# A decoder of five attention and feed-forward stages: constant matmuls as the second stage begins, its loads issued in two places, and the fifth stage's statistics in its loop

## The reference

```python
x = x + _L0_attn_ref(_layernorm(x, axis=-1), ...)
x = x + _L0_xattn_ref(_layernorm(x, axis=-1), ctx_512, ctx_512)
x = x + _L0_ffn_ref(_layernorm(x, axis=-1), ...)
x = x + _L1_attn_ref(_layernorm(x, axis=-1), ...)
x = x + _L1_xattn_ref(_layernorm(x, axis=-1), ctx_512, ctx_512, ...)
x = x + _L1_ffn_ref(_layernorm(x, axis=-1), ...)
```

## Time and profile before

| | us |
|---|---|
| median of three runs | 1947.82 |
| the profiled execution | 1944.22 |
| its span, first to last instruction | 1942.4 |
| TensorE busy | 1711.3 (88%) |
| VectorE busy | 1134.2 (58%) |
| ScalarE busy | 842.3 (43%) |
| GpSimd busy | 686.1 (35%) |
| mean granted TensorE clock | 0.902 |

### The profile page before, as it was taken

One profiled execution on the slowest core, in us unless ns is written; L12 is line 12 of the kernel. 1 busy time (PEld: TensorE's weight loads), 2 busy tenths in 40 slices (PEclk: granted clock), 3 DMA queues, 4 the chain that ended last, 5 costly groups with the idle time before them and its releaser, 6 DMA issues. The chain is left out here.

```text
span 1942.4 us, 33715 instructions
## 1 busy us (share of the span) xinstructions
PE 1711.3 (88%) x12986; PEld 1324.9 (68%) x12986; DVE 1134.2 (58%) x1820; ACT 842.3 (43%) x1399; POOL 686.1 (35%) x508
## 2 busy tenths in 40 slices
PE   4999999999959996889999786899998297999997
PEld 3888888888846665668788562444444275788886
DVE  6676767676765555565322495999897666211111
ACT  3555555555533433444422325555562275322222
POOL 0111221122123431640122204999996341223232
PEclk9999999999975555789999896999999598899999
DMA  3011111111120002000000000000000440000001
GB/s 94 15 58 55 63 38 57 54 62 38 57 98 2 1 2 92 2 2 2 2 1 1 19 18 0 1 1 1 0 1 0 157 146 2 1 1 1 1 0 43
DMA packets 49490, 57.56 MB, mean 30 GB/s; under 512 B 7216, under 2 KB 43568, under 8 KB 49248
## 3 DMA queue, kind: packets, MB, share of 16 engines
q1 hardware_dynamic: 49376, 55.97, 8.9%
HBM read 41.28 MB, written 14.68 MB: 29 GB/s over the span
## 5 line engine op out<-in xcount | busy, mean ns | idle before, releaser
L543 POOL TENSOR_TENSOR s_w_parts<-s_w_raw,s_w_parts 128x768 fp32r<-128x768 f32 x16 | 29.7, 1854 | 428.8 <-ACT s_w_parts L495 428.8
L1293 DVE TENSOR_TENSOR s6f_hid<-s6f_act_sb,s6f_u_ps 128x512 f32<-128x512 f32 x64 | 44.0, 687 | 219.5 <-PE s6f_u_ps L1244 219.5
L1316 POOL TENSOR_TENSOR s6f_hid_parts<-s6f_hid,s6f_hid_parts 128x512 fp32r<-128x512 f32 x64 | 82.7, 1293 | 230.5 <-ACT s6f_hid_parts L1282 230.5
L1826 POOL TENSOR_TENSOR s4b_pcs<-s4b_cs,s_p_rows 128x1024 f32<-128x1024 f32 x64 | 120.8, 1913 | 95.4 <-ACT s4b_cs L1872 95.4
L1837 POOL TENSOR_TENSOR s4b_with_re<-s4b_with_re,s4b_with_im 128x1024 f32<-128x1024 f32 x64 | 150.9, 2385 | 2.6 <-DVE s4b_with_im L1791 2.6
L1912 PE MATMUL s4b_c_ps<-s4b_pcs,const 128*128 128x512 f32 x256 | 122.3, 600 | 0.0
L419 PE MATMUL s_v_ps<-s_wv_parts,s_xnT 128*128 128x256 f32 x768 | 103.8, 285 | 12.0 <-ACT s_v L524 6.4
L478 PE MATMUL s_o_ps<-s_w_parts,s_zT 128*128 128x256 f32 x768 | 110.2, 294 | 4.1 <-DVE x_rows L582 4.1
L419 PEld LDWEIGHTS s_v_ps<-s_wv_parts,s_xnT 128*128 128x128 f32 x768 | 96.3, 191 | 17.6 <-ACT s_v L524 9.7
L1902 PE MATMUL s4b_turns_ps<-s_theta_bd,s_zc 128*128 128x512 f32 x128 | 78.1, 694 | 31.4 <-DVE s4b_frac L1776 30.4
L1316 POOL TENSOR_TENSOR s3f_hid_parts<-s3f_hid,s3f_hid_parts 128x512 fp32r<-128x512 f32 x32 | 41.3, 1291 | 180.2 <-ACT s3f_hid_parts L1282 180.2
(11 more groups left out here) (305 smaller groups left out, 4138.4 us busy)
## 6 DMA issues: line engine op xcount, KB each, us to landing
stored_weights<-s1q_halves SPq DMA_DIRECT2D x16, 768.0 KB, 3.5
s6w_parts<-stored_weights SPq DMA_DIRECT2D x32, 384.0 KB, 7.5
s1q_packed<-in_codes SPq DMA_DIRECT2D x8, 384.0 KB, 4.3
s1q_scale<-in_scale_rows SPq DMA_DIRECT2D x8, 384.0 KB, 5.0
x_rows<-in_x SPq DMA_DIRECT2D x1, 2048.0 KB, 8.2
s_w_raw<-in_L_attn_W_Q SPq DMA_DIRECT2D x16, 128.0 KB, 2.2
s_w_raw<-in_L_attn_W_K SPq DMA_DIRECT2D x16, 128.0 KB, 2.4
s_w_raw<-in_L_attn_W_O SPq DMA_DIRECT2D x16, 128.0 KB, 2.4
```

Source lines behind the costliest of these rows:

```text
L1293: nc.vector.tensor_tensor(hid[:, f % 2, :], act_sb[:, f % 2, :], u_ps[:, f % 2, :], ALU.mult) \
L1316: nc.gpsimd.tensor_tensor(hid_parts[:, f % 2, 1, :], hid[:, f % 2, :], hid_parts[:, f % 2, 0, :], ALU.subtract).then_inc(low_done, 1)
L1826: last = nc.gpsimd.tensor_tensor(pcs[:, half, n_, :].rearrange("p (k c) -> p k c", k=HK), cs[:, half, n_, :].rearrange("p (k c) -> p k c", ...
```

## The change

Three edits. `load_context` takes a range of chunks: the statistics block now issues chunk 0, and SyncE issues the chunks 1 to 3 in the main block of the second stage. TensorE's list in the second stage gets a part `keep_busy` at two places: ahead of all others at lag 2, with four matmuls for unit 0, and behind `scores` at lag 3, with one matmul each for the units 0 and 1. Each multiplies the constant `ident` (128x128) with the constant `age` (128x512) in float32 into `o_ps`, where nothing reads it. VectorE's list in the fifth stage gets a part `gather_stats` at lag 6, and `core.stats_ready` is set after that stage.

```diff
@@ -625,8 +625,8 @@
         loads = oroom.sems("in0", "in1", "in2", "in3")
         (zeroed,) = oroom.sems("zeroed")
 
-        def load_context(sp):
-            for n in range(NT // CHUNK):
+        def load_context(sp, first=0, last=1):
+            for n in range(first, last):
                 tiles = slice(n * CHUNK, (n + 1) * CHUNK)
                 sp.dma_start(krep[:, tiles, :, :, :].rearrange("p t r b s -> p t (r b s)"),
                              ins["ctx_rep4"][tiles, :, :].rearrange("t p n -> p t n")).then_inc(loads[n], 16)
@@ -665,6 +665,10 @@
             def attended_of():
                 return o_ps[:, 0:HEADS * (E + 1)].rearrange("p (h e) -> p h e", e=E + 1)
 
+            @block.sync
+            def _(sp):
+                load_context(sp, 1, NT // CHUNK)
+
             @block.gpsimd
             def _(pool):
                 pool.wait_ge(zeroed, 1)
@@ -763,6 +767,14 @@
             @block.tensor
             def _(pe):
                 pe.wait_ge(zeroed, 1)
+
+                def keep_busy(first, later):
+                    def part(u, rnd, n):
+                        if not isinstance(u, int) or u > 1:
+                            return
+                        for _ in range(later if u else first):
+                            nc.tensor.matmul(o_ps[:, :], core.c("ident"), core.c("age"), start=True, stop=True)
+                    return part
 
                 def turn_x(u, rnd, n):
                     i, r, k = u // 2, u % 2, u // 2 % 2
@@ -820,7 +832,7 @@
                             last.then_inc(o_full, 1)
                     return part
 
-                run_steps(pe, U, [(scores, 3), (weigh(0), 5), (turn(0), 4), (weigh(1), 5), (turn(1), 4),
+                run_steps(pe, U, [(keep_busy(4, 0), 2), (scores, 3), (keep_busy(1, 1), 3), (weigh(0), 5), (turn(0), 4), (weigh(1), 5), (turn(1), 4),
                                   (turn_x, 2)], unroll=2, head=U + 5)
 
 
@@ -944,7 +956,12 @@
                     dve.wait_ge(f_full, i + 1)
                     nc.vector.tensor_tensor(core.x[:, i, :], core.x[:, i, :], f_rows, ALU.add).then_inc(f_out, 1)
 
-            steps(dve, [(attended, 4), (shift, 2)] + ([(spread_values, 1)] if own else []) + [(finish, 5)])
+            def gather_stats(i, rnd, k):
+                dve.wait_ge(f_out, i + 1)
+                nc.vector.bn_stats(core.stats[:, i, :], core.x[:, i, :])
+
+            steps(dve, [(attended, 4), (shift, 2)] + ([(spread_values, 1)] if own else []) + [(finish, 5)] +
+                  ([] if own else [(gather_stats, 6)]))
 
         @block.gpsimd
         def _(pool):
@@ -2074,6 +2091,7 @@
 
         attention16(core, "L1", "s5a", mv, rstd, factor, {"q_cos": q_cos[:, :], "q_sin": q_sin[:, :], "shift": shift, "keys": keys, "wo": wo, "values": vbd},
                     prefetch=prefetch)
+        core.stats_ready = True
 
 
 
```

## The result

| | before | after |
|---|---|---|
| median, us | 1948.60 (4 runs, 1945.99 to 1949.42) | 1877.89 (4 runs, 1874.93 to 1880.98) |
| profiled execution, its span | 1944.22, 1942.4 | 1874.93, 1873.1 |
| mean granted clock | 0.902 | 0.952 |

What follows compares the result with a forecast made beforehand. TensorE at half clock (1.2 GHz) was taken to bound the second stage. -54.5 - 3.0 + 0.4 + 0.2 - 4.5 = -61.4 from 1944.22 gave 1882.8, carried to the median 1886; range 1874 to 1938.

Steps and rivals of the forecast that it cites:

- The clock holds: Second stage: TensorE's clock rises to 2.4 GHz and stays there to the end; chance 0.64, own range 1875 to 1898.
- the main term: Second stage's steady loop: 14.5 tile periods at full clock take 108.8 us instead of 163.3, a gain of 54.5.
- rival two: Second stage: clock never rises for the loop, or falls in the gap after the first scores; 1944 us, chance 0.17.
- the rule on transposes: The Trainium skill's rule that transposes don't count as TensorE being busy; the warm second stage would fall back, 1943 us.
- The size of a tile: Second stage's loop at full clock: 3.5 + 4.0 = 7.5 us a tile of two units, against 11.26; bounds 6.8 and 8.4.
- Filling and draining: Second stage outside the steady loop: 19.5 us, of which 3 are saved, between 0 and 6.5.
- The matmuls behind the scores: One constant matmul after each of the second stage's first two scores, mostly hidden while TensorE waits; cost 0.4 us.
- The four first: Constants ahead of the second stage's first transposes: clock rises within them, they end 4.9 to 6.5 us after beginning.
- The statistics: Fifth stage's statistics move into its loop: 5.32 - 0.75 = 4.6 us saved, taken as 4.5 (3.5 to 4.7).
- The view of before as one speed: Kernel before taken at 1944 us, its second stage at half clock; once fallen, the clock would stay down.
- Rival three: Second stage doesn't begin earlier and the constants are dead weight at 1.2 GHz: +2.5, 1950 us; chance 0.05.

Runs made afterwards that it cites:

- e5: The changed kernel with the four constant matmuls first but none behind the scores; 1937.88 us.
- e8: The changed kernel with 32 transposes of a constant in place of the first four constant matmuls; 1879.66 us.
- e6: The changed kernel without the first four constant matmuls, keeping the two behind the scores; 1877.18 us.
- e12: The kernel of e10 without the four constant matmuls at the start of the second stage; 1877.12 us.
- e11: As e1, with six constant matmuls of 256 columns ahead of the scores of units 16 and 17, in the middle of the second stage; 1917.01 us.
- e1: The changed kernel without any constant matmuls, loads and statistics as changed; 1940.65 us.
- e4: The kernel before with only the loads issued in two places; 1951.02, 1949.32, 1883.97 and 1879.79 us.
- the long runs: Executions of the unchanged kernel before: the four in the table and 22 of 33 beside the experiments, which took 1945.9 to 1952.6 us.
- the quick runs: The 11 of 33 executions of the unchanged kernel before, beside the experiments, that took 1882.7 to 1891.2 us (median 1887.2).
- e2: The kernel before with only the constant matmuls added, loads and statistics as before; 1888.13 us.
- e10: The changed kernel plus a 128-column constant matmul behind each tile's transposes, from the seventh tile, in four blocks that split x ahead of a stage; 1877.03 us.
- e9: The changed kernel run once more, unaltered; 1880.29 us.
- e7: The changed kernel with two constant matmuls instead of four ahead of the first transposes; 1878.57 us.

## Why the prediction was right, and where it was off

**The clock holds.** Right as to the time, the main term and the range (1886 against 1877.89; the sum against the profiled execution 1882.8 against 1874.93). That the times could be compared so was partly luck: had the four runs of before in the table been quick ones, the same change would have measured some 0.5%, and nothing of the main term. The gap that rival two named, put at about 1.9 us, was 1.68, and the clock held through it; without the matmul in it, it is 2.73 us, and the clock fell (e5). The weight given to the rule on transposes, little, was right (e8).

**The size of a tile** is the term that was mis-sized: 7.5 us forecast, 7.13 measured, over 14.5 tiles 5.4 of the 8 us by which the time was missed. The odd unit came as worked out (3.42 for 3.4, rounded up to 3.5). The even one was put at 4.0 for a delay in ScalarE's queue, and is 3.71: ScalarE had been idle 1.84 us when the transposes of x were done, so its copy stood behind nothing. Without the two roundings the same rows gave 7.2.

**Filling and draining** brought 4.0 us (182.78 - 118.88 = 63.9, less 14.5 x 4.13 = 59.9), net of what the two matmuls behind the scores cost; 3.0 - 0.4 = 2.6 had been forecast.

**The matmuls behind the scores** cost nothing: the first four scores follow each other every 3.42 us. The 0.4 forecast for them was too much.

**The four first** lasted 6.17 us, within the 4.9 to 6.5 forecast, and the first scores came at 578.50 in a stage that began 1.1 us later than in the trace of before (reciprocal at 571.06 against 569.95). So the start lost 0.88 - 1.11 = -0.2 us, inside -0.7 to +0.9. But the prediction took it that the clock must be up before the first transposes, and that the four bring it up. They did (576.67), but that it must be so was wrong, and the time of the changed kernel couldn't show it: e6 and e12 do without them, in eight executions of eight. So part of this was luck: what the kernels that are quick every time share is that the gaps behind the first two scores are filled, and the prediction counted these two matmuls mainly as a cost of 0.4 us.

**The statistics:** 4.6 us (7.29 to 2.65, from the last add to the square root), which the prediction worked out and took as 4.5. The -4.55 of the whole stage is the difference of two executions: over all traces that stage is 124.8 to 127.2 us with the edit and 129.5 to 130.4 without.

**The view of before as one speed.** The prediction called 1944 the time of the kernel before, and for rival two said that once down the clock stays down. But the stage has two steady speeds (e11), and which of them it gets isn't settled by its instructions (e1 and e4). The median of three runs didn't show that; a dozen very likely would have. The rival's time was right for the long runs only. Against the quick runs the change brings 1887.2 - 1877.9 = 9.3 us, of which e2's 2.6 for the loads and the 4.6 of the statistics are 7.2.

**Rival three** didn't come: GpSimd began at 572.08 and the clock was up before the first transposes.

What stays open: what decides, without the constants, between the two speeds; and the 3 to 4 us by which the third and fourth stages, which no edit touches, differ between executions (417.4 to 421.7 us for the fourth), which is why e10 against e9 can't be settled by six runs. In the same way it is open how many constants are best. From the reciprocal's end to the end of the last add the quick traces took 124.0 us (e7), 124.3 (e4, with no constant at all), 125.2 (e10), 125.5 (e8), 125.6 (e6, e12), 126.1 (after), 128.1 (e9) and 129.4 (e2, with all the loads ahead): the constants don't make the quick stage quicker, they make it come every time.

## What to carry to other kernels

A loop that is bound by TensorE at 1.2 GHz while the other engines idle may have a second steady speed: look for it in the granted clock of a loop of like build, and in the spread of the run times, before any edit. Then put spare matmuls into the gaps of the first turns, and don't rely on a block ahead of them: at half clock they last nearly twice as long (2.08 us against 1.12) and fill the gap by themselves, and once this loop ran at 2.4 GHz it needed no more. Work out the new period from the chain that binds at full clock, and don't round each link up.

## What the hardware showed beside that

- The busy time of TensorE's records doesn't tell at which clock it runs: 151.4 of 158 us at 0.50, 95.82 of 109 us at 1.00.
- The granted clock can fall near a stage's end while work goes on: in e9's profiled run at 692.95, with the last add ending 6.9 us later (699.82), and in e2's at 696.67, 3.0 us ahead of it (699.66). The windows of e9:

```profile
690.00:692.90 2.90, 2.06 (x36) 1.62 (x33) 2.63 (x4) 1.62 (x3) 0.51 (x2) 1.00 0.02 6
693.00:699.00 6.00, 5.66 (x72) 4.80 (x68) 0.81 (x3) 1.98 (x4) 0.69 (x2) 0.50 0.00 0
```

From the first scores to the end of the last add that execution took 121.0 us, and that of the same kernel in which the clock fell only after the stage's end 118.88. So the last tiles, in which fewer parts run, may be the next place for a filler; no run tried it.
